# Narrow attention on column strips: values and ones stationary, probabilities moving, and a new order inside a batch

## What is computed

```python
scores = q @ k.T * scale        # 128 x 128
prob = softmax(scores)          # rows sum to 1
z = prob @ v                    # 128 x 16 (b) or 128 x 32 (d)
y = norm(x + concat(z) @ Wo + bias)
```

## Time and profile before

| | value |
|---|---|
| median of three runs | 3754.5 us |
| profiled execution | 3771.24 us |
| its span | 3769.4 us |
| TensorE busy | 3284.9 us, 87% |
| VectorE, ScalarE, GpSimd busy | 54%, 32%, 38% |
| stage `b` | about 970 to 1500 us of the span |
| stage `d` | about 2070 to 2455 us of the span |

### The profile page before, as it was taken

How to read it: one execution, slowest core, us unless ns; L and a number is a source line. 1 busy time by engine, 2 the same in 40 slices (tenths; PEclk the granted TensorE clock), 3 DMA queues, 4 the chain that set the end, 5 groups by cost and what they waited for, 6 DMA issues and landing times. The chain is left out here.

```text
span 3769.4 us, 56030 instructions
## 1 busy us (share of the span) xinstructions
PE 3284.9 (87%) x19560; PEld 2766.9 (73%) x19560; DVE 2045.0 (54%) x3614; ACT 1215.3 (32%) x2825; POOL 1424.5 (38%) x1452
## 2 busy tenths in 40 slices
PE   7999999999699998349987899979999999739992
PEld 5878878888588887237765688758888888529892
DVE  4676575666456553401117455456767677425556
ACT  2333333333334443000110333234444444214440
POOL 3554343444211111240026222145555566255455
PEclk9999999999789997668999899989999999869996
DMA  4000040111100001402957211141101000056664
GB/s 159 17 28 34 0 130 12 44 44 61 69 19 28 21 21 45 159 3 82 340 180 169 71 36 36 34 137 33 45 11 45 11 23 11 3 188 232 236 236 150
DMA packets 129137, 301.90 MB, mean 80 GB/s; under 512 B 18602, under 2 KB 30634, under 8 KB 126467
## 3 DMA queue, kind: packets, MB, share of 16 engines
q1 hardware_dynamic: 111938, 263.14, 20.6%
q0 software_dynamic: 15360, 36.25, 3.7%
q10 hardware_dynamic: 1728, 1.07, 0.1%
HBM read 236.90 MB, written 77.60 MB: 83 GB/s over the span
## 5 line engine op out<-in xcount | busy, mean ns | idle before, releaser
L377 POOL TENSOR_TENSOR a_sq<-a_tq,a_sinq 128x256 f32<-128x256 f32 x128 | 150.1, 1191 | 356.8 <-DVE a_tq L448 356.8
L377 POOL TENSOR_TENSOR a_sk<-a_tk,a_sink 128x256 f32<-128x256 f32 x128 | 123.7, 986 | 90.0 <-DVE a_tk L448 90.0
L1609 POOL DMA_INDIRECT packed<-moe_xall,moe_rows x96 | 93.7, 977 | 158.2 <-issue 158.2
L1040 DVE TENSOR_REDUCE b_nmax<-bank 128x8 f32<-128x1024 f32 x64 | 78.4, 1224 | 138.4 <-PE bank L1169 138.3
L941 POOL TENSOR_TENSOR d_prob<-d_prob,d_nmax 128x1024 f32<-128x1024 f32 x32 | 60.9, 1904 | 232.2 <-DVE d_nmax L1038 232.2
L1190 PEld LDWEIGHTS bank<-b_va,b_probT 128*128 128x128 f32 x1024 | 140.4, 203 | 11.1 <-ACT b_probT L856 2.9
L390 POOL TENSOR_TENSOR e_sk<-e_tk 128x512 f32<-128x512 f32 x64 | 66.6, 1040 | 210.9 <-DVE e_tk L475 210.9
L343 ACT COPY a_probT<-bank 128x512 f32<-128x512 f32 x64 | 37.5, 586 | 328.5 <-PE bank L653 328.5
L335 ACT ACTIVATE e_prob<-bank,e_nb,e_rq 128x128 f32<-128x128 f32 x256 | 113.8, 455 | 83.5 <-DVE e_nb L540 83.5
L330 ACT ACTIVATE a_sm<-a_sm,a_nmax 128x128 f32<-128x128 f32 x256 | 99.8, 391 | 122.3 <-DVE a_nmax L535 122.3
L1190 PE MATMUL bank<-b_va,b_probT 128*128 128x17 f32 x1024 | 131.5, 262 | 2.0 <-ACT b_probT L856 2.0
(11 more groups left out here) (498 smaller groups left out, 10817.9 us busy)
## 6 DMA issues: line engine op xcount, KB each, us to landing
n_wg<-in_f_wg SPq DMA_DIRECT2D x24, 704.0 KB, 4.5
n_wu<-in_f_wu SPq DMA_DIRECT2D x24, 704.0 KB
cw_wg<-in_c_wg SPq DMA_DIRECT2D x32, 512.0 KB
cw_wu<-in_c_wu SPq DMA_DIRECT2D x32, 512.0 KB
cw_wd<-in_c_wd SPq DMA_DIRECT2D x32, 512.0 KB
packed<-all_zero SPq DMA_DIRECT2D x32, 384.0 KB, 4.1
n_xe<-packed SPq DMA_DIRECT2D x48, 256.0 KB
n_wd<-in_f_wd SPq DMA_DIRECT2D x24, 512.0 KB, 6.6
```

Of the source, the lines that this page charges most:

```text
L377: step = nc.gpsimd.tensor_tensor(o, i, s, ALU.mult)
L1040: nc.vector.tensor_reduce(nmax[:, p], scores, AX.X, ALU.max, negate=True).then_inc(v_nm, 1)
L1609: nc.gpsimd.indirect_dma_start(packed, bass.IndirectOffsetOnAxis(ap=rows[:, b, k:k + 1], axis=0), xall[:, b, :], None, bounds_check=bound, ...
```

## The change

**Products with V.** `probs_v` now works on two slots of heads at once. The stationary operand is a 128x32 block of `va`, and the turned probabilities move, 128 columns. Head j of a slot writes the PSUM partitions 32j to 32j+31, so four neighbouring products lie on four column strips of the array. The result is z already turned, channels by tokens. In `b`, where a head has 16 channels, `va` holds each head's values in one half of 32 columns and zeros in the other, and two heads are added into one strip (`SUBS` is 2; in `d` it is 1). The row sums come from a second set of products of the same shape with a tile `ones`, which leaves each sum on all partitions of its head. A call thus makes 16 float32 products where two calls made 8.

**Behind them.** VectorE's reciprocal and multiplication now run on 256 columns for each half of the heads, and `zn` needs no turn: `turn_z` is gone, `z_hi` and `z_lo` are made from `zn` in SBUF. The rows of Wo are permuted on the host to the new order of the channels.

**Banks and order.** "x" turns into pJ instead of pT and waits for the copy of the values of the batch before. Queries and keys have pT alone. "x" stands first in a batch on TensorE and ScalarE. In `PLAN_8` "pv" stands in every second slot, and the last two turns stand closer together; in `PLAN_4` the query projection is in one piece.

```diff
-        va = st.sbuf("va", [P, 2, NH, DH + 1])
+        va = st.sbuf("va", [P, 2, NH, W])
+        ones = st.sbuf("ones", [P, SUBS, W])
...
-        probT = st.sbuf("probT", [P, 2, H, P])
-        zn = st.sbuf("zn", [P, D])
+        probT = st.sbuf("probT", [P, 2, 2, H, P])
+        rT = st.sbuf("rT", [P, 2, 2 * P])
+        zn = st.sbuf("zn", [P, C, P])
...
             def take_z(b):
-                act.wait_ge(pe_zt, done(b))
+                for n in range(2):
+                    act.wait_ge(v_z[n], done(b))
                 act.wait_ge(pe_o, done(b - 1))
-                nc.scalar.copy(z_hi[:], pT[:, :]).then_inc(act_zt, 1)
+                nc.scalar.copy(z_hi[:], zn[:]).then_inc(act_zt, 1)
...
             def take_z(b, n):
                 dve.wait_ge(pe_z[n], done(b))
-                dve.wait_ge(pe_zt, done(b - 1))
-                z = pZ[n][:, 0:HB * (DH + 1)].rearrange("p (h d) -> p h d", h=HB)
-                nc.vector.reciprocal(rinv[:, n], z[:, :, DH]).then_inc(v_r[n], 1)
+                nc.vector.reciprocal(rT[:, n], pZ[n][:, 2 * P:4 * P]).then_inc(v_r[n], 1)
                 dve.wait_ge(v_r[n], done(b))
...
+                dve.wait_ge(v_zl, done(b - 1))
+                nc.vector.tensor_tensor(zn[:, 2 * n:2 * n + 2].rearrange("p c t -> p (c t)"), pZ[n][:, 0:2 * P], rT[:, n],
                                         ALU.mult).then_inc(v_z[n], 1)
...
             def turn_x(b):
                 pe.wait_ge(x_in, landed(b))
-                pe.wait_ge(act_t, done(2 * ROUNDS * b - 1))
+                pe.wait_ge(act_v, done(b - 1))
                 for c in range(C):
-                    last = nc.tensor.transpose(pT[:, P * c:P * c + P], xin[:, P * c:P * c + P], ident[:])
+                    last = nc.tensor.transpose(pJ[:, P * c:P * c + P], xin[:, P * c:P * c + P], ident[:])
...
             def probs_v(u, b, s, par):
-                pe.wait_ge(act_pt, done(u))
+
+                pe.wait_ge(act_pt, done(u + 1))
                 if s == 0:
                     pe.wait_ge(act_v, done(b))
...
+                for sums in (False, True):
+                    for i in range(2):
+                        blk, sub = (s + i) % (UN // 2) // SUBS, (s + i) % SUBS
+                        col = 2 * P * sums + P * blk
+                        for j in range(H):
+                            left = ones[:, sub] if sums else va[:, par, place(s + i, j)[0]]
+                            last = nc.tensor.matmul(pZ[n][W * j:W * j + W, col:col + P], left, probT[:, s // 2 % 2, i, j, :],
+                                                    start=sub == 0, stop=sub == SUBS - 1)
...
 PLAN_8 = {
     "lag": 3,
     "pe": [
-        ["s", "p", ("o2", 8, 12), "pv", "x"],
+        ["x", "s", "p", ("o2", 8, 12)],
...
-        ["s", "p", 1, "pv", ("o", 0, 4), 2],
-        ["p", "pv", 3, ("o", 4, 8)],
+        ["s", "p", ("o", 0, 2), 1, ("o", 2, 4), 2],
+        ["p", ("o", 4, 6), 3, ("o", 6, 8), "pv"],
...
 PLAN_4 = {
     "lag": 2,
     "pe": [
-        ["s", "p", ("o2", 0, 6), "x", "pv", ("o2", 6, 12)],
-        ["p", ("q", 0, 6), "pv", ("q", 6, 12)],
+        ["x", "s", "p", ("o2", 0, 6), "pv", ("o2", 6, 12)],
+        ["p", ("q", 0, 12)],
```

More of the change, by code:

```diff
@@ L688, in narrow_attention @@
     LAG = plan["lag"]
-    in_order = [e for slot in plan["pe"] for e in slot if e == "zt" or isinstance(e, int)]
-    TURNS_BEFORE_Z = in_order.index("zt")
+    SUBS = W // DH
     with ExitStack() as ctx:
@@ L757, in narrow_attention @@
         n_const = 16 * (3 if rope else 1)
+        n_made = 3 + SUBS * SUBS + (2 if rope else 0)
         block = ctx.enter_context(nc.Block())
@@ L825, in take_x @@
                     act.wait_ge(pe_v, done(b - 1))
-                nc.scalar.copy(x_hi[:], pT[:, :]).then_inc(act_x, 1)
+                nc.scalar.copy(x_hi[:], pJ[:, :]).then_inc(act_x, 1)
             def take_context(b):
@@ L845, in take_v @@
                 act.wait_ge(pe_z1, done(b - 2))
-                nc.scalar.copy(va[:, par, :, 0:DH], heads(pJ[:, :], NH)).then_inc(act_v, 1)
+                if SUBS == 1:
+                    nc.scalar.copy(va[:, par], heads(pJ[:, :], NH)).then_inc(act_v, 1)
+                    return
+                quarters = va[:, par].rearrange("p (g t) w -> p g (t w)", t=2).rearrange("p g (f d) -> p g f d", d=DH)
+                nc.scalar.copy(quarters[:, :, 0:4:3, :], heads(pJ[:, :], NH).rearrange("p (g t) d -> p g t d", t=2)).then_inc(act_v, 1)
             def take_t(b, par, n):
@@ L855, in take_prob @@
                 act.wait_ge(pe_pt, done(u))
-                nc.scalar.copy(probT[:, s % 2], pP[:, :]).then_inc(act_pt, 1)
+                nc.scalar.copy(probT[:, s // 2 % 2, s % 2], pP[:, :]).then_inc(act_pt, 1)
             def exponent(w, p):
@@ L863, in slot @@
                 u = UN * b + s
+                if s == 0 and ahead:
+                    take_x(b + 1)
                 if s % 2:
@@ L868, in slot @@
                 for e in plan["act"][s]:
-                    if e == "x" and ahead:
-                        take_x(b + 1)
                     if e == "c" and ahead:
@@ L901, in _ @@
             nc.gpsimd.memset(mhalf[:], -0.5).then_inc(g_c, 1)
-            nc.gpsimd.memset(va[:], 1.0).then_inc(g_c, 1)
+            nc.gpsimd.memset(va[:], 0.0).then_inc(g_c, 1)
+            for t in range(SUBS):
+                for r in range(SUBS):
+                    nc.gpsimd.memset(ones[:, t, DH * r:DH * r + DH], 1.0 if r == t else 0.0).then_inc(g_c, 1)
             nc.gpsimd.memset(eps[:], EPS).then_inc(g_c, 1)
@@ L906, in _ @@
                 nc.gpsimd.memset(ks[:], 0.0).then_inc(g_c, 1)
-            pool.wait_ge(g_c, 5 if rope else 3)
+            pool.wait_ge(g_c, n_made)
             pool.wait_ge(c_in, n_const)
@@ L1181, in probs_v @@
             def probs_v(u, b, s, par):
-                pe.wait_ge(act_pt, done(u))
+                pe.wait_ge(act_pt, done(u + 1))
                 if s == 0:
                     pe.wait_ge(act_v, done(b))
-                if s in (0, UN // 2):
-                    pe.wait_ge(v_z[2 * s // UN], done(b - 1))
-                for j in range(H):
-                    h = place(s, j)[0]
-                    col = ((H * s + j) % HB) * (DH + 1)
-                    last = nc.tensor.matmul(pZ[2 * s // UN][:, col:col + DH + 1], probT[:, s % 2, j, :], va[:, par, h, :],
-                                            start=True, stop=True)
-                if s in (UN // 2 - 1, UN - 1):
-                    last.then_inc(pe_z[2 * s // UN], 1)
-            def turn_z(b, ahead=True):
-                for n in range(2):
-                    pe.wait_ge(v_z[n], done(b))
-                pe.wait_ge(v_xl, done(b + 2 if ahead else B - 1))
-                pe.wait_ge(act_t, done(2 * ROUNDS * (b + 2) + TURNS_BEFORE_Z - 1 if ahead else 2 * ROUNDS * B - 1))
-                for c in range(C):
-                    last = nc.tensor.transpose(pT[:, P * c:P * c + P], zn[:, P * c:P * c + P], ident[:])
-                last.then_inc(pe_zt, 1)
+                n = 2 * s // UN
+                if s % (UN // 2) == 0:
+                    pe.wait_ge(v_z[n], done(b - 1))
+                for sums in (False, True):
[6 more added lines that the diff above has]
+                                                    start=sub == 0, stop=sub == SUBS - 1)
+                if s + 2 in (UN // 2, UN):
+                    last.then_inc(pe_z[n], 1)
             def output(b, parts, ahead=True):
@@ L1220, in slot @@
                         turn_prob(u - LAG, (s - LAG) % UN)
-                    if what == "pv" and (back or s >= LAG + 1):
-                        s1 = (s - LAG - 1) % UN
-                        here = s >= LAG + 1
-                        probs_v(u - LAG - 1, b if here else b - 1, s1, par if here else 1 - par)
+                    if what == "pv" and (back or s >= LAG + 2):
+                        here = s >= LAG + 2
+                        probs_v(u - LAG - 2, b if here else b - 1, (s - LAG - 2) % UN, par if here else 1 - par)
                     if ahead:
@@ L1235, in slot @@
                             turn(b + 1, what)
-                    if back and what == "zt":
-                        turn_z(b - 1, ahead)
                     if back and what == "o":
@@ L2385, in layout_shared, with in_slots @@
             "ident": np.eye(P, dtype=np.float32)}
+def in_slots(w, NH):
+    d = D // NH
+    if d == 16:
+        return w.reshape(2, 4, 2, 2, d, D).transpose(0, 2, 1, 3, 4, 5).reshape(D, D)
+    return w.reshape(4, 4, d, D).transpose(1, 0, 2, 3).reshape(D, D)
 def layout_l0_xattn(i):
@@ L2405, in layout_l1_attn @@
         "d_wq": by_chunk(w[:D].T), "d_wk": by_chunk(w[D:2 * D].T), "d_wv": by_chunk(w[2 * D:].T),
-        "d_wo": by_chunk(i["L1_attn_weight_out"].T), "d_mask": np.where(seen, 0.0, NEG).astype(np.float32),
+        "d_wo": by_chunk(in_slots(i["L1_attn_weight_out"].T, 16)), "d_mask": np.where(seen, 0.0, NEG).astype(np.float32),
     }
```

43 lines of the change are left out of this document (17 added, 26 removed), and 4 rows, old and new, of tables (PLAN_4, PLAN_8).

## The result

The kernel after takes 3660.2 us, the median of four runs (3657.03 to 3663.66); the kernel before, measured beside it four times, takes 3752.49. The ratio is 0.9756 with a 95% interval of 0.9739 to 0.9773: 92 us faster. The forecast was 77 us faster, 3677, and its range of 3652 to 3752 holds the time.

The account below looks back on a forecast made before the run. TensorE's stream was taken to bound the kernel; b's batch falling 28.72 to 24.74 us (60 us over 15 distances) and d's 21.32 to 20.2 (17) gave 77 us off 3754.5, hence 3677, range 3652 to 3752.

Parts of the forecast that it names:

- TensorE bounds the kernel before: Whole kernel: stages b and d run at the pace of TensorE's stream, busy 3284.9 of 3769.4 us.
- The visit, 1.30 us: TensorE, b and d: 16 products on four column strips side by side cost 1.30 us, replacing two groups, 1.76.
- My lower bound, 1.2: TensorE: a visit below 1.2 us was excluded, since eight matmuls of 128 columns follow one another on each strip.
- the rival of 2.15 us: TensorE: strips run two at a time, 2.15 us a visit, 3752 us in all; with what lies between, chance 0.20.
- Nothing side by side: TensorE: no strips overlap, 3.85 us a visit, 3906 us in all; with any other loss, chance 0.12.
- The reciprocal, 1747 ns: VectorE, b and d: 256 elements take 1747 ns, 1.5 us more than before, twice a batch.
- It stays under TensorE: VectorE grows to 19.9 us a batch in b and 14.6 in d, yet stays below TensorE's time.
- the 0.5 allowed for turn 2 and late probabilities: TensorE, b: 0.4 us a batch waiting for turn 1's copy, 0.1 for turns of probabilities behind a late copy.
- The wait for x_lo and its half clock: TensorE, b: a 1.13 us wait goes, and with it half-clock stretches worth 0.65 us a batch.
- d: Stage d: batch falls from 21.32 to 20.2 us, including a new 0.88 us wait before the turn of x.
- more than that: Rival, b's first 120 us: denser work lifts the clock from 0.76, winning 10 to 15 us more, 3663; no separate chance.
- The clock takes it back: Rival, d: the new 0.88 us wait sets off half clock, 0.65 us a batch, 3687 in all; no separate chance.

Follow-up runs that it names:

- visits_split: Kernel after, with each visit to the column strips split: values' products, then other TensorE work, then the sums' products; 3682.2 us.
- before_x_first: Kernel before, with only x (TensorE's turn, ScalarE's and VectorE's copies) moved to the head of slot 0 in b; 3724.7 us.
- b_x_late: Kernel after, with x in b alone (TensorE's turn and its copies) put back where the kernel before had it; 3662.4 us.

## Why the prediction was right, point by point

- **TensorE bounds the kernel before**: right. Moving x alone took out the wait, and the batch fell by it and the half clock behind it.
- **The visit, 1.30 us**: right in kind, too dear by 0.19. TensorE's own stream is 23.85 us with turn 2's 0.37, so four visits are 23.85 - 0.37 - 19.04 = 4.44, 1.11 each, as in the timeline. My lower bound, 1.2, was too high as well: I had added the 0.35 of the scores in full to eight paces of 0.112, and it measures 0.30 (visits_split, in d) or less. Strips in parallel are shown (eight loads in 0.10 us), and so is the condition, which the prediction did not name: two strips at a time, the rival of 2.15 us, is what comes out (at 2.5) when the products of a strip stand in a row.
- **Nothing side by side**: refuted. What the page "TensorE: Matmul & The Clock Gate" of the Trainium skill states (row and column tiling), that a load overlaps matmuls in flight only where the row group differs, does not hold for these strips, which share all rows: 12 matmuls and 8 loads touch one 0.10 us, and a visit takes 1.11 us where 32 steps of 0.109, one behind another, would take 3.5.
- **The reciprocal, 1747 ns**: exact (1744 in b, 1757 in d). The estimate of 2.13 us from the repeat count of 8 in the page "VectorE: DVE Perf Modes" of the Trainium skill (the fixed hardware budget) was too long; the slope from 8 to 16 elements carried to 256.
- **"It stays under TensorE"**: wrong for b, and this is the step that failed. I had compared busy time, 19.9 of 24.7 us, and named the scores' maximum as late. But VectorE's work has no gap between x_lo and the last scores, and closes a ring through TensorE's second half of the batch. The ring cost 1.0 us a batch, 15 us: with a short reciprocal (23.85) or the same one in the idle time (23.89) it is gone. It cancelled against the visits that were too dear (4 x 0.19) and the rest of the 0.5 allowed for turn 2 and late probabilities (0.13), together 0.9, which is why 24.74 met 24.84. That the sum for b came out is luck: one price too high and one wait left out. In d it was right: the pace is TensorE's, and 3.5 us more on VectorE cost 1.03, by the late keys that the prediction had named.
- **The wait for x_lo and its half clock**: right before, 1.71 us a batch by before_x_first against 1.78 forecast. In the sum I took it as one term among others; it is worth that only while nothing else holds the batch.
- **d**: batch 19.94 against 20.2, the new wait 0.94 against 0.88. Not seen: d's first three batches, which before waited 2.6 us for x_lo and then ran at clock 0.84 (a later batch, without either, is in the earlier trace rows); they are 12.6 us shorter in all, where my 1.1 each made 3.4. The other part that the forecast lacked is the clock in b's first 120 us, the rival "more than that": PEclk 0.79 to 0.91 over the first four batches, which are 25.2 us shorter in all, where my 4.0 each made 16. In the profiles each of the two is worth some 9 us; how they share the 15 us between 77 and 92 is not settled, since the profiled execution of before was a long one (the three distances of d, unchanged there, are 2.1 us shorter in before_x_first).
- **The clock takes it back**: did not happen; PEclk is 1.00 in d's middle with a wait of 0.94 in every batch.

How much of the profiles' 114 us, of b's end above all, belongs to that one execution of before, which was 18.8 us longer than its median, stays open.

## What to carry to other kernels

Price an engine against the ring it stands in, not against its share of the time: follow one batch from a step back to the same step of the next, through every engine, and see what work has no gap on the way. Here an engine that was busy for 80% of a batch set its length. If an added operation stands before something that the leading engine waits for, move it into the idle time ahead of the step that waits (here 2.2 us into 4.3), and look at what is queued behind it on the engine that takes its result. Four small products ran together where neighbours in the program go to different strips; put the loop over strips innermost (1.11 us a visit against 2.5).

## What was not expected of the hardware

- Four column strips of float32 products (32 stationary, 128 moving columns) each keep a pace of 0.11 us for a record, all four together; a visit of 32 matmuls and 32 loads took 1.11 us. Ordered strip by strip, the same ones take 2.5, as if TensorE reached past one strip's waiting products to a second strip, not to the third and fourth; how it chooses no run shows.
- Going into and out of column strips once more cost 0.30 us in d, whose pace is TensorE's.
- A wait of 0.9 to 1.1 us was followed by half clock in the kernel before, but neither in b_x_late, with a wait as long in each batch of b, nor in d after the change. What decides between them no run here told apart.
